# Second layer norm and router logits of a vision-transformer tower: logits token by token, rows normalised on ScalarE, moments a block ahead

## The chip, the cores and the metric

The program runs on one core of a Trainium2 chip. The metric is the device time of one execution in microseconds (us); the median of a few runs is quoted. The engines of a core are TensorE (PE; its weight loads are shown as PEld), VectorE (DVE), ScalarE (ACT), GpSimd (POOL) and SyncE (SP), which here issues the DMA transfers.

## The reference

64 images give 12544 tokens of 256 channels. A token embedding is followed by a 16-head attention block and then by a feed-forward block of one shared expert and eight routed ones, each block on a layer-normed copy of the rows. The change lies in what stands ahead of the feed-forward block:

```python
m = jnp.mean(x, axis=axis, keepdims=True)
v = jnp.var(x, axis=axis, keepdims=True)
return (x - m) / jnp.sqrt(v + eps)
...
z = xf @ proj_w.T + proj_b
s = jax.nn.sigmoid(z) + expert_bias
```

`x` are the rows h1 that attention left in DRAM (12544 x 256, f32), `xf` the normed rows, `proj_w` is 8 x 256. Then come the choice of two experts per token, the capacity cut of each expert, and the experts.

## The kernel before

The program is a row of stages with a barrier after each: `project` (embedding, first layer norm, Q, K, V), `attend`, `route`, and three `feed_forward` stages. The change touches `route` alone. Each engine has its own instruction list in the source; what orders them are semaphores, and inside an engine the order is as written.

`route` first walks over the tokens in 28 blocks of 4 tiles of 112 tokens (`BLOCKS`, `BLOCK`, `GROUP`; N = 448 tokens), and then works out the expert tables from the logits of all tokens, `z`. The walk is the function `position(n, u)`, once per engine, called for n from -2 to 27; the middle positions run in a hardware loop of two. In one position the engines do this:

- SP waits for the normed rows of block n+2, loads the input of block n+4 (L1563) into the buffer that they came from, and stores the normed rows (L1581).
- DVE takes the moments of block n+2 (`bn_stats` L1654, `bn_aggr` L1660, four each), waits for ScalarE's square root, takes the reciprocal (L1663), writes the normed rows `xf` (L1668, four instructions), and last adds the bias to the logits of block n (L1673).
- ACT takes the square root for block n+2 (L1602), copies the 8 x 448 logits of block n+1 out of PSUM (`zT`, L1606), and copies the transposed rows of block n+2 out of PSUM (`xT`, L1609).
- PE multiplies for block n+1 with the 128 x 8 router weights as the stationary operand and the 448 tokens streaming (`psZ`, L1842, two f32 products, each two records in the trace), turns the logits of block n back to token-major with four small transposes (`psB`, L1849), and transposes the rows of block n+2 with eight (`psT`, L1856).

`xT` and `psT` are single buffers: the transposes of a block wait until `xT` of the block before has been copied (L1609), and that copy waits for the transposes of its own block. `hin` (the input) and `xf` have two buffers each. In the rest of the text Z is the product into `psZ`, B the small transposes into `psB`, and T the eight transposes into `psT`. Two other places of the program are read for their durations: L469 in `project`, eight products with `prod` (128 x 98 tokens) as the stationary operand and 8 streaming columns, sixteen records in all, and L1868 in `route`, a 128 x 128 stationary operand with one column.

Of the kernel before, what the change touches and what calls it, by code (L numbers as in the profile page):

```python
# [20 lines left out]
C = 256  # L21
# [1006 lines left out]
BLOCK = 4  # L1028
# [439 lines left out]
def route(nc, d, networks):  # L1468
# [5 lines left out]
    with stage(nc) as ctx:  # L1474
# [12 lines left out]
        def plain(x):  # L1487
# [9 lines left out]
        hin = [sb(f"hin{u}", [GROUP, BLOCK, C]) for u in range(2)]  # L1497
        xf = [sb(f"xf{u}", [GROUP, BLOCK, C]) for u in range(2)]
        stats, mv = sb("stats", [GROUP, BLOCK, 6]), sb("mv", [GROUP, BLOCK, 2])
        std, rstd = sb("std", [GROUP, BLOCK]), sb("rstd", [GROUP, BLOCK])  # L1500
        xT, zT = sb("xT", [128, 2, N]), sb("zT", [EXPERTS, N])
# [22 lines left out]
        psZ, psB, psC = pb("psZ", [EXPERTS, 512]), pb("psB", [GROUP, BLOCK, EXPERTS]), pb("psC", [GROUP, EXPERTS])  # L1524
# [8 lines left out]
        h_in, xf_out = transfers("h1_in"), transfers("xf_out")  # L1533
        stats_ok, mv_ok, std_ok, rstd_ok, xf_ok = (signal(x) for x in ("stats", "mv", "std", "rstd", "xf"))
        t_ok, xT_ok, z_ok, zT_ok, zz_ok, zw_ok = (signal(x) for x in
                                                 ("xT_in_psum", "xT", "z_in_psum", "zT", "z_transposed", "z"))
# [9 lines left out]
        def positions(eng, position):  # L1546

            for n in (-2, -1, 0, 1):
                position(n, n % 2)
            with eng.Fori(1, BLOCKS // 2 - 2) as j:  # L1550
                for u in range(2):
                    position(j * 2 + u, u)
            for n in range(BLOCKS - 4, BLOCKS):
                position(n, n % 2)

        with nc.Block() as block:
            @block.sync
            def _(sp):
                for s in (h_in, xf_out):
                    s.open(sp)  # L1560

                def load(n, u):
                    sp.dma_start(hin[u][:], tiles_of(d["h1"][bass.ds(n * N, N), :], GROUP)).then_inc(h_in.sems[u], 16)  # L1563

                load(0, 0)
                load(1, 1)
                for dst, name in ((ident, "ident"), (wz, "proj_w"), (bz, "proj_b"), (eb, "expert_bias"), (iota, "iota"),
                                  (rows0, "rows0"), (tri32, "tri"), (blk8, "blk8")):
                    sp.dma_start(dst[:], d[name]).then_inc(setup, 16)

                for x, raw in zip(networks, raws):
                    for dst, src in ((raw[0], "w1"), (raw[1], "w2"), (x.b1, "b1"), (x.b2, "b2")):
                        sp.dma_start(dst[:], d[x.source + src][0]).then_inc(w_in, 16)

                def position(n, u):
                    if known(n, -2, BLOCKS - 2):
                        sp.wait_ge(xf_ok.sem, xf_ok.at(n + 2))
                        sp.sem_inc(passed["sp"], 1)
                        if known(n, -2, BLOCKS - 4):
                            load(n + 4, u)  # L1580
                        sp.dma_start(tiles_of(d["xf"][bass.ds((n + 2) * N, N), :], GROUP), xf[u][:]).then_inc(xf_out.sems[u], 16)  # L1581

                positions(sp, position)
                sp.wait_ge(xf_out.sems[0], xf_out.at(BLOCKS - 2, 0))
                sp.wait_ge(xf_out.sems[1], xf_out.at(BLOCKS - 1, 1))

                sp.wait_ge(tables_ready, 1)
                for name, src in (("gidx", gidx), ("gw", gw), ("sidx", sidx)):
                    sp.dma_start(d[name], src[:]).then_inc(tables_out, 16)
                sp.wait_ge(tables_out, 48)  # L1590

            @block.scalar
            def _(act):
                for s in (std_ok, xT_ok, zT_ok):
                    s.open(act)
                act.wait_ge(made, 1)

                def position(n, u):
                    if known(n, -2, BLOCKS - 2):
                        act.wait_ge(mv_ok.sem, mv_ok.at(n + 2))  # L1600
                        act.wait_ge(rstd_ok.sem, rstd_ok.at(n + 1))
                        act.activation(std[:], mv[:, :, 1], ACT.Sqrt, bias=eps[:, 0:1]).then_inc(std_ok.sem, 1)  # L1602
                    if known(n, -1, BLOCKS - 1):
                        act.wait_ge(z_ok.sem, z_ok.at(n + 1))
                        act.wait_ge(zz_ok.sem, zz_ok.at(n))
# [26 lines left out]
            def _(dve):  # L1632
                for s in (stats_ok, mv_ok, rstd_ok, xf_ok, zw_ok):
                    s.open(dve)
# [15 lines left out]
                def position(n, u):  # L1650
                    if known(n, -2, BLOCKS - 2):
                        dve.wait_ge(h_in.sems[u], h_in.at(n + 2, u))
                        for t in range(BLOCK):
                            last = nc.vector.bn_stats(stats[:, t, :], hin[u][:, t, :])  # L1654
                        last.then_inc(stats_ok.sem, 1)
                        dve.wait_ge(stats_ok.sem, stats_ok.at(n + 2))
                        dve.wait_ge(std_ok.sem, std_ok.at(n + 1))
                        dve.sem_inc(passed["dve"], 1)
                        for t in range(BLOCK):
                            last = nc.vector.bn_aggr(mv[:, t, :], stats[:, t, :])  # L1660
                        last.then_inc(mv_ok.sem, 1)
                        dve.wait_ge(std_ok.sem, std_ok.at(n + 2))
                        nc.vector.reciprocal(rstd[:], std[:]).then_inc(rstd_ok.sem, 1)  # L1663
                        dve.wait_ge(rstd_ok.sem, rstd_ok.at(n + 2))
                        dve.wait_ge(xf_out.sems[u], xf_out.at(n, u))
                        dve.wait_ge(t_ok.sem, t_ok.at(n))
                        for t in range(BLOCK):
                            last = nc.vector.tensor_scalar(xf[u][:, t, :], hin[u][:, t, :], mv[:, t, 0:1], rstd[:, t:t + 1],  # L1668
                                                           ALU.subtract, ALU.mult)
                        last.then_inc(xf_ok.sem, 1)  # L1670
                    if known(n, 0, BLOCKS):
                        dve.wait_ge(zz_ok.sem, zz_ok.at(n))
                        nc.vector.tensor_tensor(z[:, bass.ds(n * BLOCK, BLOCK), :], psB[:],  # L1673
                                                         bz[:].unsqueeze(1).broadcast_to([GROUP, BLOCK, EXPERTS]), ALU.add).then_inc(zw_ok.sem, 1)
# [156 lines left out]
            def _(pe):  # L1831
                for s in (t_ok, z_ok, zz_ok):
# [4 lines left out]
                def position(n, u):  # L1837
                    if known(n, -1, BLOCKS - 1):
                        pe.wait_ge(xT_ok.sem, xT_ok.at(n + 1))
                        pe.wait_ge(zT_ok.sem, zT_ok.at(n))  # L1840
                        for h in range(2):
                            last = nc.tensor.matmul(psZ[:, 0:N], wz[:, h, :], xT[:, h, :], start=(h == 0), stop=(h == 1))  # L1842
                        last.then_inc(z_ok.sem, 1)
                    if known(n, 0, BLOCKS):
                        pe.wait_ge(zT_ok.sem, zT_ok.at(n))
                        pe.wait_ge(zw_ok.sem, zw_ok.at(n - 1))
                        pe.sem_inc(passed["pe"], 1)
                        for t in range(BLOCK):
                            last = nc.tensor.transpose(psB[:, t, :], zT[:, t * GROUP:(t + 1) * GROUP], ident[0:EXPERTS, 0:EXPERTS])  # L1849
                        last.then_inc(zz_ok.sem, 1)  # L1850
                    if known(n, -2, BLOCKS - 2):
                        pe.wait_ge(xf_ok.sem, xf_ok.at(n + 2))
                        pe.wait_ge(xT_ok.sem, xT_ok.at(n + 1))
                        for h in range(2):
                            for t in range(BLOCK):
                                last = nc.tensor.transpose(psT[:, h, t * GROUP:(t + 1) * GROUP], xf[u][:, t, h * 128:(h + 1) * 128],  # L1856
# [137 lines left out]
```

## Time and profile before

| | us |
|---|---|
| median of 3 runs | 3623.16 (3621.2 to 3627.92) |
| the profiled execution, time | 3636.08 |
| the profiled execution, span | 3634.4 |

The page of the profiled execution gives busy times, shares of the span and instruction counts of the engines:

```profile
span 3634.4 us, 89293 instructions
PE 3229.9 (89%) x34825; PEld 2526.0 (70%) x34881; DVE 2623.7 (72%) x6129; ACT 1498.6 (41%) x2991; POOL 1617.8 (45%) x1965
```

The 40 equal slices of the span (90.9 us each) show the stages; a digit is a tenth of busy time, 9 is 90% or more, and PEclk is the granted clock of TensorE in tenths of full speed:

```profile
PE   6999999399999999999996722999599999998997
DVE  5888888568888888888884676554266666665887
ACT  3444444056666666666663310332133333332221
PEclk9999999579999999999998855999799999998999
```

The walk of `route` lies in slices 22 and 23 (counted from 1), 1966 to 2110 us; the work on the tables follows to 2250 us. What the profile calls the granted clock is 1.00 at 2.4 GHz and 0.50 at 1.2 GHz.

### The profile page before, as it was taken

What the parts mean: (1) busy time and instruction counts of PE and PEld (TensorE: products, weight loads), DVE (VectorE), ACT (ScalarE), POOL (GpSimd) and SP (SyncE); (2) the same over time, 40 slices, a digit from 0 to 9 for tenths busy, and PEclk for the clock granted to TensorE, in tenths of its full rate; (3) what the DMA queues carried; (4) which work ended last, traced back from release to release, by engine and by line L of the source; (5) the groups of instructions that cost most, each with busy time, mean ns of one, the idle gap of its engine ahead of it and who ended that gap; (6) DMA issues with size and microseconds to landing.
All of it is one profiled execution on the core that took longest, in us unless ns stands there. A gap on an engine that the chain in (4) does not pass through costs nothing. (4 is left out here: it accounts for less than half of the span.)

```text
span 3634.4 us, 89293 instructions
## 1 busy us (share of the span) xinstructions
PE 3229.9 (89%) x34825; PEld 2526.0 (70%) x34881; DVE 2623.7 (72%) x6129; ACT 1498.6 (41%) x2991; POOL 1617.8 (45%) x1965
## 2 busy tenths in 40 slices
PE   6999999399999999999996722999599999998997
PEld 6888887378888888888883311778377777775876
DVE  5888888568888888888884676554266666665887
ACT  3444444056666666666663310332133333332221
POOL 2555555256666666666662010577200000004776
PEclk9999999579999999999998855999799999998999
DMA  4666665736556565665654611354333333225776
GB/s 141 185 185 197 195 186 161 189 84 164 157 149 172 136 166 148 160 162 148 170 133 131 182 30 34 110 140 126 95 116 111 107 104 106 95 90 135 217 219 165
DMA packets 449244, 518.11 MB, mean 143 GB/s; under 512 B 64150, under 2 KB 418804, under 8 KB 448397
## 3 DMA queue, kind: packets, MB, share of 16 engines
q1 hardware_dynamic: 427376, 473.19, 46.1%
q0 software_dynamic: 21504, 39.94, 4.1%
q8 instruction: 245, 4.01, 0.5%
q14 instruction: 119, 0.97, 0.1%
HBM read 306.93 MB, written 215.94 MB: 144 GB/s over the span
## 5 line engine op out<-in xcount | busy, mean ns | idle before, releaser
L1281 POOL DMA_INDIRECT sb_ye<-scratch_ye,sb_table x224 | 240.8, 1075 | 805.6 <-DMA sb_gw<-scratch_gw 733.3
L854 DVE TENSOR_REDUCE p_mx<-p_psS 98x2 f32<-98x390 f32 (+1 forms) x1024 | 527.1, 556 | 0.0
L800 ACT ACTIVATE p_after<-p_psF 98x392 f32<-98x392 f32 x512 | 255.1, 498 | 480.6 <-PE p_psF L946 472.5
L803 ACT ACTIVATE p_probs<-p_psE 98x392 f32<-98x392 f32 x1024 | 450.1, 496 | 0.0
L848 DVE COPY_PREDICATED p_psS<-p_later,p_psD 98x196 f32<-98x196 uint32 x1024 | 330.6, 362 | 120.0 <-PE p_psS L932 111.4
L749 POOL TENSOR_SCALAR_AFFINE_SELECT p_after<-p_after 98x392 f32<-98x392 f32 x512 | 274.4, 536 | 243.2 <-ACT p_after L800 243.0
L1269 POOL DMA_INDIRECT scratch_xe<-sa_xs,sa_table x224 | 222.2, 992 | 205.6 <-DMA sa_xs<-scratch_xf 140.4
L753 POOL TENSOR_SCALAR_AFFINE_SELECT p_probs<-p_probs 98x392 f32<-98x392 f32 x512 | 274.5, 536 | 85.8 <-ACT p_probs L803 80.2
L969 PE MATMUL p_psO<-p_probs,p_v 98*32 98x196 f32 x4096 | 279.8, 345 | 2.0 <-POOL p_probs L753 1.7
L419 POOL TENSOR_TENSOR p_rt<-p_rt 128x784 f32<-128x784 f32 x64 | 187.1, 2924 | 122.7 <-DVE p_st L397 122.7
L103 PE MATMUL p_psH<-p_wh,p_xh 128*98 128x256 bf16 x768 | 211.5, 275 | 24.3 <-DVE p_xl L334 24.3
L916 PE MATMUL p_psD<-p_K,p_U 96*98 96x98 bf16 (+1 forms) x2048 | 187.8, 215 | 36.7 <-DVE p_later L835 29.0
L916 PEld LDWEIGHTS p_psD<-p_K,p_U 96*98 96x98 bf16 x2048 | 160.6, 128 | 73.4 <-DVE p_later L835 29.1
L103 PE MATMUL p_psH<-p_wl,p_xh 128*98 128x256 bf16 x768 | 211.3, 275 | 0.0
L103 PE MATMUL p_psH<-p_wh,p_xl 128*98 128x256 bf16 x768 | 211.2, 275 | 0.0
L946 PE MATMUL p_psF<-p_U,p_K 98*98 98x98 bf16 x2048 | 180.3, 211 | 28.8 <-DMA p_U<-p_mrow 28.8
L1387 DVE CAST ex_gh<-ex_g 128x512 bf16<-128x512 f32 (+1 forms) x256 | 106.3, 415 | 106.7 <-ACT ex_g L1322 87.4
L973 PE MATMUL p_psO<-p_after,p_v 98*32 98x98 f32 x4096 | 182.3, 250 | 0.0
L1389 DVE TENSOR_TENSOR ex_gl<-ex_g,ex_gh 128x512 bf16<-128x512 f32 (+1 forms) x256 | 171.4, 669 | 8.8
L1322 ACT ACTIVATE ex_g<-ex_psG,ex_b 128x512 f32<-128x512 f32 (+1 forms) x128 | 85.7, 669 | 219.7 <-PE ex_psG L103 219.7
L1322 ACT ACTIVATE ex_g<-ex_psG,ex_first_b 128x512 f32<-128x512 f32 (+1 forms) x128 | 85.7, 669 | 218.1 <-PE ex_psG L103 218.1
L946 PEld LDWEIGHTS p_psF<-p_U,p_K 98*98 98x98 bf16 x2048 | 147.5, 127 | 32.5 <-DMA p_U<-p_mrow 31.6
(300 smaller groups left out, 10110.7 us busy)
## 6 DMA issues: line engine op xcount, KB each, us to landing
scratch_stack<-p_st SPq DMA_DIRECT2D x64, 784.0 KB, 6.0
p_x<-in_x SPq DMA_DIRECT2D x32, 1176.0 KB, 9.5
p_L<-scratch_stack SPq DMA_DIRECT2D x192, 196.0 KB, 4.3
p_U<-scratch_stack SPq DMA_DIRECT2D x192, 196.0 KB, 4.4
scratch_xe<-p_zero SPq DMA_DIRECT2D x32, 1024.0 KB, 5.9
ex_xin<-scratch_xe SPq DMA_DIRECT2D x56, 512.0 KB, 4.0
scratch_ye<-ex_y SPq DMA_DIRECT2D x56, 512.0 KB
scratch_h<-p_h SPq DMA_DIRECT2D x32, 392.0 KB
```

Of the source, the lines that this page charges most:

```text
L103: last = nc.tensor.matmul(out, a, b, start=start and k == 0, stop=stop and k == len(todo) - 1)
L749: nc.gpsimd.affine_select(after[c][:], after[c][:], pattern=[[0, 4], [-1, TILE]], compare_op=ALU.is_ge, fill=nothing, base=-2, channel_mul ...
L753: nc.gpsimd.affine_select(diagonal, diagonal, pattern=[[0, 4], [1, TILE]], compare_op=ALU.is_ge, fill=nothing, base=0, channel_multiplier= ...
L800: act.activation(after[c][:].rearrange("p h t -> p (h t)"), psF[:, 0:4 * TILE], ACT.Exp, scale=DK ** -0.5).then_inc(p_ok.sem, 1)
L803: act.activation(probs[c][:, b, :], psE[:, b, 0:PAIR], ACT.Exp, scale=DK ** -0.5).then_inc(p_ok.sem, 1)
L848: nc.vector.copy_predicated(own[:, :, c * TILE:(c + 1) * TILE], later[:].unsqueeze(1).broadcast_to([TILE, 2, TILE]), upper).then_inc(chose ...
L854: nc.vector.tensor_reduce(mx[g1][:, c, 4 * q1 + 2 * b:4 * q1 + 2 * b + 2], own, AX.X, ALU.max).then_inc(s_max.sem, 1)
L916: last = nc.tensor.matmul(psD[:, j * TILE:j * TILE + wide], U[u][0:STACK, h][:, mid], K[u][0:STACK, h][:, mid.start + 1:mid.start + 1 + wi ...
L946: last = nc.tensor.matmul(psF[:, j * TILE:(j + 1) * TILE], K[u][0:ROWS, h][:, mid], U[u][0:ROWS, h][:, mid], start=True, stop=True)
L969: nc.tensor.matmul(psO[32 * j:32 * j + 32, 0:S], v32[u][:, 2 * g + c, 4 * q + j, :], probs[c][:, j // 2, (j % 2) * S:(j % 2 + 1) * S], sta ...
L1269: nc.gpsimd.indirect_dma_start(out=d["xe"], out_offset=bass.IndirectOffsetOnAxis(ap=table[:, b * BLOCK + t, k:k + 1], axis=0), in_=xs[v][: ...
L1281: nc.gpsimd.indirect_dma_start(out=ye[v][u][:, t, k, :], out_offset=None, in_=d["ye"], in_offset=bass.IndirectOffsetOnAxis(ap=table[:, at ...
```

## The change

All of it is in the walk of `route`.

- **Logits.** The operands of Z change places: the transposed rows `xT`, 112 tokens at a time, are now the stationary operand, and the 8 columns of `wz` stream. That makes 8 products per block in place of 2, and the result is already token-major, so B, the copy `zT` on ScalarE and their semaphores go. `psZ` is now 112 x 4 x 8 and has two buffers.
- **Rows.** `xf` is written by ScalarE, `rstd * h - mean * rstd`, four instructions with a bias and a scale per partition. DVE makes `nmr = -mean * rstd` with one small instruction after the reciprocal.
- **Order.** The moments are taken at position n for block n+4, the rows are written for block n+3; so positions run from -4. On ScalarE the order in a position is rows of n+3, square root of n+4, copy `xT` of n+2. On PE it is Z of n+1, T of n+3. Small buffers (`mv`, `std`, `rstd`, `nmr`) are double.
- **Input.** Four `hin` buffers; blocks 2 and 3 are loaded before the experts' weights, and a load is issued for n+7 at position n.
- **Loop.** The hardware loop is gone; all positions are written out.

```diff
-        hin = [sb(f"hin{u}", [GROUP, BLOCK, C]) for u in range(2)]
+        hin = [sb(f"hin{v}", [GROUP, BLOCK, C]) for v in range(4)]
...
-            for n in (-2, -1, 0, 1):
-                position(n, n % 2)
-            with eng.Fori(1, BLOCKS // 2 - 2) as j:
...
+            for n in range(-4, BLOCKS):
                 position(n, n % 2)
...
+                    if known(n, -3, BLOCKS - 3):
+                        v = 1 - u
+                        act.wait_ge(rstd_ok.sem, rstd_ok.at(n + 3))
+                        act.wait_ge(xf_out.sems[v], xf_out.at(n + 1, v))
+                        act.wait_ge(t_ok.sem, t_ok.at(n + 1))
+                        for t in range(BLOCK):
+                            last = act.activation(xf[v][:, t, :], hin[(n + 3) % 4][:, t, :], ACT.Identity, bias=nmr[v][:, t:t + 1],
+                                                  scale=rstd[v][:, t:t + 1])
+                        last.then_inc(xf_ok.sem, 1)
...
-                        act.activation(zT[:], psZ[:, 0:N], ACT.Copy).then_inc(zT_ok.sem, 1)
                     if known(n, -2, BLOCKS - 2):
                         act.wait_ge(t_ok.sem, t_ok.at(n + 2))
+                        act.wait_ge(z_ok.sem, z_ok.at(n + 1))
                         act.activation(xT[:], psT[:, :, 0:N], ACT.Copy).then_inc(xT_ok.sem, 1)
...
+                        nc.vector.scalar_tensor_tensor(nmr[v][:], mv[v][:, :, 0], -1.0, rstd[v][:], ALU.mult, ALU.mult).then_inc(rstd_ok.sem, 1)
...
-                        for t in range(BLOCK):
-                            last = nc.vector.tensor_scalar(xf[u][:, t, :], hin[u][:, t, :], mv[:, t, 0:1], rstd[:, t:t + 1],
-                                                           ALU.subtract, ALU.mult)
-                        last.then_inc(xf_ok.sem, 1)
...
                         pe.wait_ge(xT_ok.sem, xT_ok.at(n + 1))
-                        pe.wait_ge(zT_ok.sem, zT_ok.at(n))
-                        for h in range(2):
-                            last = nc.tensor.matmul(psZ[:, 0:N], wz[:, h, :], xT[:, h, :], start=(h == 0), stop=(h == 1))
+                        pe.wait_ge(zw_ok.sem, zw_ok.at(n - 1))
+                        for t in range(BLOCK):
+                            for h in range(2):
+                                last = nc.tensor.matmul(psZ[1 - u][:, t, :], xT[:, h, t * GROUP:(t + 1) * GROUP], wz[:, h, :],
+                                                        start=(h == 0), stop=(h == 1))
                         last.then_inc(z_ok.sem, 1)
-                    if known(n, 0, BLOCKS):
-                        pe.wait_ge(zT_ok.sem, zT_ok.at(n))
-                        pe.wait_ge(zw_ok.sem, zw_ok.at(n - 1))
                         pe.sem_inc(passed["pe"], 1)
-                        for t in range(BLOCK):
-                            last = nc.tensor.transpose(psB[:, t, :], zT[:, t * GROUP:(t + 1) * GROUP], ident[0:EXPERTS, 0:EXPERTS])
-                        last.then_inc(zz_ok.sem, 1)
```

## Rows read from the trace of the kernel before

**Rows 1.** Windows over the walk: length, busy of five engines, granted clock, DMA share, GB/s.
```profile
1966.00:2109.60 143.60, 98.36 (x448) 41.90 (x448) 96.78 (x394) 51.30 (x86) 0.00 (x0) 0.85 0.64 195
```
**Rows 2.** Timeline, two neighbouring blocks: start, length, engine, line, operation, [idle before <-releaser].
```profile
2095.82 1.67 PE L1842 MATMUL p_psZ<-p_xT,p_wz 128*8 128x448 f32 x4 [1.01 <-ACT p_xT L1609]
2097.41 0.38 PE L1849 MATMUL p_psB<-p_ident,p_zT 8*112 8x8 f32 x4
2098.22 0.99 PE L1856 MATMUL p_psT<-p_ident,p_xf 112*128 112x112 f32 x8 [0.43 <-DVE p_xf L1668]
2099.25 0.92 ACT L1609 ACTIVATE p_xT<-p_psT 128x896 f32<-128x896 f32 x1 [0.82 <-PE p_psT L1856]
...
2100.22 3.01 PE L1842 MATMUL p_psZ<-p_xT,p_wz 128*8 128x448 f32 x4 [1.01 <-ACT p_xT L1609]
...
2103.16 0.54 PE L1849 MATMUL p_psB<-p_ident,p_zT 8*112 8x8 f32 x4
2103.63 1.05 PE L1856 MATMUL p_psT<-p_ident,p_xf 112*128 112x112 f32 x8
```
**Rows 3.** Waits in the walk: who waited for whom, total us, times, longest us.
```profile
PE p_psZ L1842 <- ACT p_xT L1609: 29.1, 28, 1.1
PE p_psT L1856 <- DVE p_xf L1668: 8.6, 13, 0.9
DVE p_stats L1654 <- DMA p_hin<-scratch_h: 1.0, 2, 0.7
```
**Rows 4.** Timeline, start of the walk: the first T, copy and Z, and their neighbours.
```profile
1966.50 1.40 DVE L1654 BATCH_NORM_STATS2 p_stats<-p_hin 112x6 f32<-112x256 f32 x4
1968.08 0.38 DVE L1660 BATCH_NORM_AGGREGATE p_mv<-p_stats 112x2 f32<-112x6 f32 x4 [0.17 <-DVE p_stats L1654]
1969.82 0.30 ACT L1602 ACTIVATE p_std<-p_mv,p_eps 112x4 f32<-112x4 f32 x1
1970.15 0.18 DVE L1663 RECIPROCAL p_rstd<-p_std 112x4 f32<-112x4 f32 x1 [1.70 <-ACT p_std L1602]
...
1972.01 1.73 PE L1856 MATMUL p_psT<-p_ident,p_xf 112*128 112x112 f32 x8 [20.45 <-DVE p_xf L1668]
1973.77 0.92 ACT L1609 ACTIVATE p_xT<-p_psT 128x896 f32<-128x896 f32 x1 [3.65 <-PE p_psT L1856]
1974.74 3.03 PE L1842 MATMUL p_psZ<-p_xT,p_wz 128*8 128x448 f32 x4 [1.01 <-ACT p_xT L1609]
```
**Rows 5.** Timeline, end of the walk.
```profile
2105.69 1.67 PE L1842 MATMUL p_psZ<-p_xT,p_wz 128*8 128x448 f32 x4 [1.01 <-ACT p_xT L1609]
...
2109.61 0.95 ACT L1613 ACTIVATE p_c<-p_z 112x896 f32<-112x896 f32 x1
```
**Rows 6.** Timeline of PE in `project`: L469 at clock 0.50, then at 1.00.
```profile
639.67 2.83 PE L469 MATMUL p_psT<-p_blk,p_prod 128*98 128x8 f32 x16 [6.34 <-DVE p_nl L363]
202.33 1.47 PE L469 MATMUL p_psT<-p_blk,p_prod 128*98 128x8 f32 x16
```
**Rows 7.** Timeline of PE in the tables: one product, 128 x 128 stationary, one column.
```profile
2134.14 0.58 PE L1868 MATMUL p_psK<-p_count_of,p_same 128*128 128x1 f32 x2 [2.05 <-DVE p_hits L1742]
```
**Rows 8.** Windows of PE alone in the walk: length, busy (records), granted clock, DMA share, GB/s.
```profile
1970.80:1974.10 3.30, 1.73 (x8) 0.50 1.04 374
1974.20:1977.50 3.30, 2.76 (x4) 0.50 0.95 286
1977.60:1981.00 3.40, 2.39 (x13) 1.00 0.87 245
...
1998.10:2001.40 3.30, 1.38 (x10) 1.00 0.49 121
2001.50:2004.80 3.30, 3.30 (x11) 0.50 0.83 246
```
**Rows 9.** Windows of PE alone in `project` (L469) and `attend`.
```profile
639.60:642.90 3.30, 3.23 (x19) 0.50 0.59 180
643.00:646.30 3.30, 3.30 (x17) 0.50 0.08 8
656.70:660.00 3.30, 2.23 (x14) 0.50 0.82 249
660.10:663.40 3.30, 0.51 (x4) 0.50 0.08 8
740.00:760.00 20.00, 20.00 (x223) 0.50 0.17 55
```
**Rows 10.** Groups of ACT: count, busy us, mean ns, idle before.
```profile
L309 ACT ACTIVATE p_st<-p_psJ,p_cols 128x392 bf16<-128x392 f32 x64 | 37.6, 587 | 53.6 <-PE p_psJ L103 53.6
L1606 ACT ACTIVATE p_zT<-p_psZ 8x448 f32<-8x448 f32 x28 | 14.9, 534 | 57.4 <-PE p_psB L1849 54.5 <-PE p_psZ L1842 2.9
```

More of the change, by code:

```diff
@@ L1496, in route @@
         tri, ones = sb("tri", [GROUP, GROUP], BF16), sb("ones", [GROUP, GROUP], BF16)
-        hin = [sb(f"hin{u}", [GROUP, BLOCK, C]) for u in range(2)]
+        hin = [sb(f"hin{v}", [GROUP, BLOCK, C]) for v in range(4)]
         xf = [sb(f"xf{u}", [GROUP, BLOCK, C]) for u in range(2)]
-        stats, mv = sb("stats", [GROUP, BLOCK, 6]), sb("mv", [GROUP, BLOCK, 2])
-        std, rstd = sb("std", [GROUP, BLOCK]), sb("rstd", [GROUP, BLOCK])
-        xT, zT = sb("xT", [128, 2, N]), sb("zT", [EXPERTS, N])
+        stats, mv = sb("stats", [GROUP, BLOCK, 6]), [sb(f"mv{u}", [GROUP, BLOCK, 2]) for u in range(2)]
+        std, rstd, nmr = ([sb(f"{x}{u}", [GROUP, BLOCK]) for u in range(2)] for x in ("std", "rstd", "nmr"))
+        xT = sb("xT", [128, 2, N])
         z, c, key, oh1, oh2, c2, w, t1, t2 = (sb(x, wide) for x in
@@ L1523, in route @@
         psT = pb("psT", [128, 2, 512])
-        psZ, psB, psC = pb("psZ", [EXPERTS, 512]), pb("psB", [GROUP, BLOCK, EXPERTS]), pb("psC", [GROUP, EXPERTS])
+        psZ, psC = [pb(f"psZ{u}", [GROUP, BLOCK, EXPERTS]) for u in range(2)], pb("psC", [GROUP, EXPERTS])
         psK = pb("psK", [128, 512])
@@ L1532, in route @@
         setup, made = plain("constants_loaded"), plain("constants_made")
[L1533 to L1536, printed above, removed]
+        h_in, xf_out = [plain(f"h1_in{v}") for v in range(4)], transfers("xf_out")
+        stats_ok, mv_ok, std_ok, recip_ok, rstd_ok, xf_ok = (signal(x) for x in ("stats", "mv", "std", "reciprocal", "rstd_and_shift", "xf"))
+        t_ok, xT_ok, z_ok, zw_ok = (signal(x) for x in ("xT_in_psum", "xT", "z_in_psum", "z"))
         sig_ok = plain("sigmoid")
@@ L1558, in _, with load @@
             def _(sp):
[L1559 to L1566, printed above, removed]
+                xf_out.open(sp)
+                def load(n):
+                    sp.dma_start(hin[n % 4][:], tiles_of(d["h1"][bass.ds(n * N, N), :], GROUP)).then_inc(h_in[n % 4], 16)
+                load(0)
+                load(1)
                 for dst, name in ((ident, "ident"), (wz, "proj_w"), (bz, "proj_b"), (eb, "expert_bias"), (iota, "iota"),
@@ L1569, in _ @@
                     sp.dma_start(dst[:], d[name]).then_inc(setup, 16)
+                load(2)
+                load(3)
                 for x, raw in zip(networks, raws):
@@ L1593, in _ @@
             def _(act):
-                for s in (std_ok, xT_ok, zT_ok):
+                for s in (std_ok, xf_ok, xT_ok):
                     s.open(act)
@@ L1598, in position @@
                 def position(n, u):
[L1599 to L1605, printed above, removed]
-                        act.activation(zT[:], psZ[:, 0:N], ACT.Copy).then_inc(zT_ok.sem, 1)
+                    if known(n, -3, BLOCKS - 3):
+                        v = 1 - u
[6 more added lines that the diff above has]
+                        last.then_inc(xf_ok.sem, 1)
+                    if known(n, -4, BLOCKS - 4):
+                        act.wait_ge(mv_ok.sem, mv_ok.at(n + 4))
+                        act.wait_ge(rstd_ok.sem, rstd_ok.at(n + 2))
+                        act.activation(std[u][:], mv[u][:, :, 1], ACT.Sqrt, bias=eps[:, 0:1]).then_inc(std_ok.sem, 1)
                     if known(n, -2, BLOCKS - 2):
                         act.wait_ge(t_ok.sem, t_ok.at(n + 2))
+                        act.wait_ge(z_ok.sem, z_ok.at(n + 1))
                         act.activation(xT[:], psT[:, :, 0:N], ACT.Copy).then_inc(xT_ok.sem, 1)
@@ L1632, in _ @@
             def _(dve):
-                for s in (stats_ok, mv_ok, rstd_ok, xf_ok, zw_ok):
+                for s in (stats_ok, mv_ok, recip_ok, rstd_ok, zw_ok):
                     s.open(dve)
@@ L1650, in position @@
                 def position(n, u):
-                    if known(n, -2, BLOCKS - 2):
-                        dve.wait_ge(h_in.sems[u], h_in.at(n + 2, u))
+                    if known(n, -3, BLOCKS - 3):
+                        v = 1 - u
+                        dve.wait_ge(std_ok.sem, std_ok.at(n + 3))
+                        dve.wait_ge(xf_ok.sem, xf_ok.at(n + 1))
+                        nc.vector.reciprocal(rstd[v][:], std[v][:]).then_inc(recip_ok.sem, 1)
+                        dve.wait_ge(recip_ok.sem, recip_ok.at(n + 3))
+                        nc.vector.scalar_tensor_tensor(nmr[v][:], mv[v][:, :, 0], -1.0, rstd[v][:], ALU.mult, ALU.mult).then_inc(rstd_ok.sem, 1)
@@ L1653, in position @@
+                    if known(n, -4, BLOCKS - 4):
+                        v = (n + 4) % 4
+                        dve.wait_ge(h_in[v], 16 * ((n + 4) // 4 + 1))
+                        dve.wait_ge(mv_ok.sem, mv_ok.at(n + 3))
                         for t in range(BLOCK):
-                            last = nc.vector.bn_stats(stats[:, t, :], hin[u][:, t, :])
+                            last = nc.vector.bn_stats(stats[:, t, :], hin[v][:, t, :])
                         last.then_inc(stats_ok.sem, 1)
-                        dve.wait_ge(stats_ok.sem, stats_ok.at(n + 2))
@@ L1657, in position @@
-                        dve.wait_ge(std_ok.sem, std_ok.at(n + 1))
+                        dve.wait_ge(stats_ok.sem, stats_ok.at(n + 4))
+                        dve.wait_ge(rstd_ok.sem, rstd_ok.at(n + 2))
                         dve.sem_inc(passed["dve"], 1)
                         for t in range(BLOCK):
-                            last = nc.vector.bn_aggr(mv[:, t, :], stats[:, t, :])
+                            last = nc.vector.bn_aggr(mv[u][:, t, :], stats[:, t, :])
                         last.then_inc(mv_ok.sem, 1)
-                        dve.wait_ge(std_ok.sem, std_ok.at(n + 2))
@@ L1670, in position @@
-                        last.then_inc(xf_ok.sem, 1)
                     if known(n, 0, BLOCKS):
-                        dve.wait_ge(zz_ok.sem, zz_ok.at(n))
-                        nc.vector.tensor_tensor(z[:, bass.ds(n * BLOCK, BLOCK), :], psB[:],
-                                                         bz[:].unsqueeze(1).broadcast_to([GROUP, BLOCK, EXPERTS]), ALU.add).then_inc(zw_ok.sem, 1)
+                        dve.wait_ge(z_ok.sem, z_ok.at(n))
+                        nc.vector.tensor_tensor(z[:, n * BLOCK:(n + 1) * BLOCK, :], psZ[u][:],
+                                                bz[:].unsqueeze(1).broadcast_to([GROUP, BLOCK, EXPERTS]), ALU.add).then_inc(zw_ok.sem, 1)
@@ L1831, in _ @@
             def _(pe):
-                for s in (t_ok, z_ok, zz_ok):
+                for s in (t_ok, z_ok):
                     s.open(pe)
```

24 lines of the change are left out of this document (8 added, 16 removed).

## The prediction

> **What bounds the kernel now.** I read the windows first. The walk takes 143.6 us, 4% of the span, and in it no engine is full: PE 98.36 us, DVE 96.78, ACT 51.30, DMA share 0.64, granted clock 0.85 [rows 1]. So latencies round a loop set the pace, and the timeline shows which: Z, B and T follow one another on PE, the copy `xT` (0.92 us) waits for T, and the next Z waits for that copy [rows 2]. From the first Z at 1974.74 [rows 4] to the last at 2105.69 [rows 5] there are 27 periods in 130.95 us, 4.85 us each. The waits agree: PE stood 29.1 us for `xT` (28 times, the 0.92 us and hand-overs) and only 8.6 us for DVE's rows [rows 3]. Periods come in two kinds. At clock 1.00 Z takes 1.67 us and a period 4.40 (2095.82 to 2100.22, with 0.43 us of waiting for rows); at 0.50 Z takes 3.01 and the period is 5.47 (2100.22 to 2105.69) [rows 2, 5]. The reader should see that PE plus the copy is the loop, DVE is second with small waits, and the clock is the large term.
>
> **Which clock the new work gets.** This decides the sum, so it comes first. In before, the stage begins at 0.50; eight transposes alone (1.73 us busy) left it there; after a Z of long streams it rose to 1.00 for T, B and Z; after a stretch with the late start of a Z and otherwise only transposes (1.38 us busy) it fell [rows 8]. So it is the 448-column streams of Z that bring the clock up, and the change takes just these away: new Z streams 16 times 8 columns. The nearest rows to that are L469, sixteen records with 8 streaming columns, at 0.50: after 14 of them (2.23 us busy) and after all 16 with a few others (3.23 of 3.30 us busy) the next stretch was still at 0.50. In `attend` PE was busy for 20.00 of 20.00 us at 0.50, so a busy record does not raise it by itself [rows 9]. I therefore take 0.50 for the whole walk. The Trainium skill (TensorE: Matmul & The Clock Gate, Part 4) says that transposes do not count as busy for the clock; by that rule too T could not bring it up, and the first T above, which left the clock at 0.50, agrees.
>
> **The change, part by part, per block.**
>
> B goes: 0.38 us at 1.00, 0.54 at 0.50 [rows 2]. Copy `zT` (0.534 us, rows 10) lay beside PE and on nobody's path but B's; its removal gives ScalarE room only.
>
> Z, new: 16 records with a stationary operand of 128 x 112 and 8 columns. L469 has the same form with 98 token columns: 2.83 us for 16 at 0.50, 1.47 at 1.00 [rows 6]. Loading the stationary operand sets this, since the streams are 8 columns; it scales with token columns: the 128-column product has two records in 0.58 us, so a spacing of about 0.22 against (2.83 - 0.34) / 15 = 0.166 for 98 columns, taking 0.34 for the last record [rows 6, 7]. For 112 columns I scale 2.83 by 112/98 to 3.2 us. Bounds: 2.83 (no scaling) and 16 x 0.215 = 3.44. At 1.00 it would be 1.47 x 112/98 = 1.7, the same as the old Z's 1.67. So the exchange of operands is free at full clock and, without clock, costs what the old slow Z cost (3.03, rows 4).
>
> T is unchanged, at 0.50 it takes 1.73 us [rows 4], 0.99 at 1.00 [rows 2]. Z's first load begins about 0.26 us before T's last record ends (spacing 0.183, last record some 0.45), so T's share before Z is 1.47; bound 1.73.
>
> Copy `xT`: 0.92 us, now on both T of its block and Z of the block before; hand-overs 0.05 before and 0.08 after it [rows 2]. PE now does T(n+2), Z(n+1), and waits for `xT`(n+2), so the period is 1.47 + 3.2 + 0.03 + 0.92 + 0.13 = 5.75 us against 4.85.
>
> What lies beside that period: ScalarE writes four row tiles. The nearest row, 128x392 with one per-partition operand, takes 587 ns [rows 10]; 136 elements fewer at 0.855 ns (from 917 ns for 896 and 534 for 448 elements, rows 2, 10) gives 470 ns. With overlap or a second operand I take 1.9 to 2.2 us for four; plus the square root, 0.30. Queued behind them on ScalarE is `xT`(n+2), which waits 4.7 us for PE anyway, so this costs nothing; if PE ran at full clock (T + Z = 2.5 us), 2.5 us of ScalarE would just fill it. DVE loses four row instructions and has 1.40 + 0.38 + 0.18 plus a small one for `nmr` (0.18, by the reciprocal) and the bias add: under 3 us, hidden. The wait for rows (8.6 us in all, rows 3) disappears; it is within the 4.85. DMA moves the same bytes in a longer period, and the earlier loads remove at most 1.0 us of waiting [rows 3]. On SP a load for n+7 stands ahead of the store as before and both wait only for the rows. Loop instructions go; written out, they lie behind PE's waits: nothing, with at most 3 us either way.
>
> **Sum.** 27 periods x (5.75 - 4.85) = +24.3 us. Start: before, the first `xT` ended at 1974.69. Now ScalarE does rows(0), then rows(1) and the square root of block 2 before it: square root(0) to 1970.12, reciprocal and `nmr` to 1970.75, rows(0) to 1972.8, square root(1) to 1973.1, `nmr`(1) 1973.8, rows(1) 1975.8, square root(2) 1976.1, `xT`(0) to 1977.05: +2.4. End: before, 3.92 us from the last Z's start to the sigmoid [rows 5]; now Z 3.2, bias add 0.2, hand-over 0.1: -0.4. Together +26.3. Against the profiled execution's own 3636.08 that is 3662.4; it stands 12.9 above the median of the runs, so by the median 3623.16 + 26.3 = 3649.5 us, +0.73%. Bounds from Z (-10, +6.5) and T (+7) and 3 us for code and runs: 3637 to 3664.
>
> **Rivals.**
>
> *The clock is 1.00 as soon as PE has shorter gaps.* Then Z is 1.7, T's share 0.8: a period of 0.8 + 1.7 + 0.95 + 0.13 = 3.6; ScalarE's 2.2 + 0.3 + 0.92 with hand-overs is about as long, so 3.7. 27 x (3.7 - 4.85) = -31, start and end +1: 3593, faster. Everything hangs on TensorE's clock: PE's work per period is denser than before (gaps of 1.1 us only), which speaks for it; rows 8 and 9 speak against. The turn is at a period of about 4.8, so with half of the blocks at each clock (5.75 and 3.7, mean 4.7) the gain is gone.
>
> *The clock alternates as it does before.* Then 27 x (4.7 - 4.85) + 2 = -2: 3621, no change.
>
> *A load is shorter than I take it.* At 0.50, if a load took as long as it does at 1.00 (1.47 / 16 = 0.09 us a record, rows 6), Z would be 1.7 us and the period 4.25: 27 x (-0.6) + 1 = -15, 3608. The Trainium skill (TensorE: Matmul & The Clock Gate, Part 2, LDWEIGHTS) gives a load as columns divided by 1.2 in ns, 93 ns for 112 columns, whatever the clock, which is this case. L469 took nearly twice as long at 0.50 as at 1.00, so the trace contradicts it for f32.
>
> *The change does not unload PE at all in the sense that counts:* DVE's rows and the input buffers were worth 8.6 + 1.0 us at most [rows 3]; this part does what it says but is covered by PE's longer phase. That is part of the forecast.
>
> **How the numbers follow.** Chance of the forecast (0.50 throughout) 0.84; clock 1.00 throughout 0.05; alternating 0.07; short loads 0.04. A measurement of this kernel can tell about 0.2%, 7 us, from no change. Slower by over that: 0.83; within: 0.07; faster: 0.10. The range 3637 to 3664 is that of the forecast and holds it nine times in ten; the other cases are left out as they are less than 2 in 10.
>
> **What would show it.** After: granted clock 0.50 in all windows of the walk, Z near 3.2 us for 16 records, T 1.73, a period of 5.75, no wait of PE for rows, the walk some 26 us longer, and ScalarE waiting for PE ahead of `xT`. It is wrong if the windows show 1.00 (then look for periods of 3.7), if Z's sixteen records take under 2.5 us at 0.50, or if `xT` waits behind the row instructions of ScalarE rather than for PE.

## The result

| | us |
|---|---|
| before, median of 4 runs | 3625.54 (3621.2 to 3629.04) |
| after, median of 4 runs | 3654.69 (3651.31 to 3658.19) |
| after / before | 1.0081, 95% interval 1.0065 to 1.0097 |
| profiled execution of after, time (span) | 3656.93 (3655.2) |

The change makes the kernel 0.81% slower; 3649.5 us and +0.73% were forecast. The page of after (parts 1 and 2, engines by line) stands against the one of before:

```profile
PE 3255.7 (89%) x35049; PEld 2608.3 (71%) x35105; DVE 2586.8 (71%) x6045; ACT 1533.9 (42%) x3075; POOL 1618.8 (44%) x1965
...
PE   6999999499999999999995732999599999998997
...
DVE  5888888478888888888873366555266666665987
ACT  3444444056666666666664510332133333332221
...
PEclk9999999589999999999995555999799999998999
```

DVE lost 36.9 us of busy time and ScalarE gained 35.3, as the change means to; TensorE's weight loads gained 82 us. The clock digits of slices 22 and 23 went from 8 and 8 to 5 and 5. The stretch from the first moments to the sigmoid is the walk. Windows over it (busy of PE, PEld, DVE, ACT, POOL with records, then granted clock, DMA share, GB/s), whole and without its first blocks:

```profile
1958.20:2127.50 169.30, 127.50 (x672) 125.34 (x672) 62.45 (x309) 88.70 (x170) 0.00 (x0) 0.50 0.54 164
1980.00:2127.50 147.50, 117.26 (x619) 115.45 (x619) 50.73 (x253) 76.50 (x146) 0.00 (x0) 0.50 0.48 143
```

In before it ran from 1966.50 to 2109.61 [rows 4, 5], 143.1 us at 0.85 [rows 1]; now it takes 169.3 us at 0.50: +26.2 us. The rest of the difference is outside the change: in the two profiled executions the part ahead of the walk was 8.3 us shorter after the change (1958.2 against 1966.5) and the part behind it 2.9 us longer (1527.7 against 1524.8), though its code is the same. In the fourteen profiled kernels of this study the part ahead spread from 1953.7 to 1966.5 us. So below I read the walk from traces and the sign of a change from the ratio of runs. The low clock is not that of one execution: averaged over the whole span it was 0.922 to 0.924 in the four runs of after, and 0.938 to 0.944 in the runs of before that went with the experiments.

One block of after in the timeline (start, length, engine, line, operation, [idle before <-releaser]):

```profile
1981.47 2.06 ACT L1600 ACTIVATE p_xf<-p_hin,p_nmr,p_rstd 112x256 f32<-112x256 f32 x4
1981.69 1.41 PEld L1853 LDWEIGHTS p_psT<-p_ident,p_xf 112*128 112x128 f32 x8 [1.22 <-issue]
1981.72 1.73 PE L1853 MATMUL p_psT<-p_ident,p_xf 112*128 112x112 f32 x8 [1.16 <-ACT p_xT L1610]
1983.05 3.11 PEld L1844 LDWEIGHTS p_psZ<-p_wz,p_xT 128*112 128x112 f32 x16
1983.24 3.02 PE L1844 MATMUL p_psZ<-p_wz,p_xT 128*112 128x8 f32 x16
1983.43 0.29 ACT L1606 ACTIVATE p_std<-p_mv,p_eps 112x4 f32<-112x4 f32 x1
1986.36 0.92 ACT L1610 ACTIVATE p_xT<-p_psT 128x896 f32<-128x896 f32 x1 [2.63 <-PE p_psZ L1844]
```

The next T starts at 1987.42, 5.70 us after this one. The weight loads of Z fill 3.11 us, the eight-column streams hide behind them, and ScalarE, done with its rows and its square root at 1983.72, stands 2.63 us until Z is done. The waits (who for whom: us in total, times, longest) say the same of the walk from 1975 us on:

```profile
ACT p_xT L1610 <- PE p_psZ L1844: 70.8, 26, 4.8
...
PE p_psT L1853 <- ACT p_xT L1610: 32.2, 26, 3.3
```

PE no longer waits for rows behind the first block (8.6 us in rows 3). The long wait is now ScalarE's for PE, ahead of `xT`.

### The profile page after: what moved, and what is told of

It is laid out like the page before. It is cut to its first block and busy times, and to the rows that moved or that the text cites. A ratio compares the mean times of both kernels' runs of the same rounds, so it can differ in the third digit from the quotient of the medians.

```text
span 3655.2 us, 89450 instructions
## 1 busy us (share of the span) xinstructions
PE 3255.7 (89%) x35049; PEld 2608.3 (71%) x35105; DVE 2586.8 (71%) x6045; ACT 1533.9 (42%) x3075; POOL 1618.8 (44%) x1965
## 5 line engine op out<-in xcount | busy, mean ns | idle before, releaser
L916 PEld LDWEIGHTS p_psD<-p_K,p_U 96*98 96x98 bf16 x2048 | 160.1, 128 | 72.6 <-DVE p_later L835 29.2
```

The lines of the kernel that those rows point to most:

```text
L916: last = nc.tensor.matmul(psD[:, j * TILE:j * TILE + wide], U[u][0:STACK, h][:, mid], K[u][0:STACK, h][:, mid.start + 1:mid.start + 1 + wi ...
```

## The experiments

The theory: TensorE's clock stays at 0.50 because the change takes the long streams of Z away; at that clock Z costs its sixteen weight loads, and they lie on the chain. Rivals: rows on ScalarE or the new order are the cost; the clock has nothing to do with the streams; the stretch has another limit right behind. Every ratio is against the kernel before on the same chip.

### The logits alone, in the kernel before

```diff
-                        for h in range(2):
-                            last = nc.tensor.matmul(psZ[:, 0:N], wz[:, h, :], xT[:, h, :], start=(h == 0), stop=(h == 1))
+                        for t in range(BLOCK):
+                            for h in range(2):
+                                last = nc.tensor.matmul(psZ[1 - u][:, t, :], xT[:, h, t * GROUP:(t + 1) * GROUP], wz[:, h, :],
+                                                        start=(h == 0), stop=(h == 1))
```

> The kernel before with the logits part alone: xT stationary, 8 columns streaming, no zT and no small transposes; DVE still writes the rows, two input buffers, hardware loop. Theory: clock 0.50 throughout, the same PE loop of T 1.47 + Z 3.0 + xT 0.92 and hand-overs, DVE's 4.2 us per block hidden in it: period 5.7, time within 4 us of the changed kernel (3650 to 3658). Rival A (the order of the change costs too): clearly less than that, by 5 us or more. Rival C (the loop and DVE's rows add to the longer PE phase): over 3660.

Measured: 3657.57 us, ratio 1.0076 (1.006 to 1.0093), the same as the whole change (1.0081). The walk:

```profile
1961.10:2131.80 170.70, 132.07 (x672) 123.10 (x672) 94.09 (x393) 33.52 (x58) 0.00 (x0) 0.50 0.54 161
```

170.7 us at 0.50 with DVE still at 94 us, against 169.3: this part alone brings all of the loss, and the rows and the order of the change give back next to nothing while PE is this long. Inside they are not quite without effect. A block takes 5.90 us here (T at 1989.91 and 1995.81 in the timeline) against the 5.70 expected and measured in after; after loses most of those 27 x 0.2 us again in its first blocks, as told below.

### Half of the products

```diff
-                            for h in range(2):
+                            for h in range(1):
                                 last = nc.tensor.matmul(psZ[1 - u][:, t, :], xT[:, h, t * GROUP:(t + 1) * GROUP], wz[:, h, :],
-                                                        start=(h == 0), stop=(h == 1))
+                                                        start=True, stop=True)
```

This leaves out half of the channels, so the logits are others; only the walk is read from it.

> The changed kernel with the second half of the channels left out of the logits (4 products per block, 8 records instead of 16), so the logits are of half the channels. Theory (Z is priced by its loads at 0.50 and lies wholly on the chain): 8 x 0.19 = 1.5 us less per block, period 5.70 to 4.2, the walk 41 us shorter, time 3613. Rival (another wait is right behind): less than 30 us.

Measured: 3617.28 us, ratio 0.9965 (0.9954 to 0.9975). The window over the walk:

```profile
1955.90:2085.70 129.80, 85.69 (x448) 83.53 (x448) 59.88 (x309) 88.79 (x171) 0.00 (x0) 0.50 0.72 214
```

The clock is 0.50 as in after, but the walk is 39.5 us shorter than 169.3, against 41 forecast, and a block takes 4.21 us against 4.2. The loads of Z, at the price of the low clock, lie on the chain nearly one for one.

### Unread streams on TensorE

Products that nobody reads, 448 bf16 columns each, behind Z in the changed kernel; first four per block, then eight.

```diff
                         last.then_inc(z_ok.sem, 1)
                         pe.sem_inc(passed["pe"], 1)
+                        for _ in range(8):
+                            nc.tensor.matmul(psU[:, 0, 0:448], ones[:], stream[:], start=True, stop=True)
```

> The changed kernel plus four bf16 products per block with 448 streaming columns (112x112 ones stationary) behind Z on PE, whose results nobody reads; they fill the stretch in which PE waits for xT. Theory: streams are what the clock lacks. If four (0.75 us at 1.00) are enough, clock 1.00, T share 0.83, Z 1.6, period 3.5 to 3.7, time near 3598. If they are too few, they cost 4 x 0.373 = 1.5 us at 0.50 in a gap of 1.1: period 6.1, time near 3666. Rival (clock does not follow streams): the second outcome here and with eight too.

> As with four streams, but eight per block. Theory: clock 1.00, the eight take 1.5 us of PE, 0.4 us more than the gap: period 3.9 to 4.1, time near 3610. Rival (clock does not follow streams): 8 x 0.373 = 3.0 us at 0.50, period 7.6, time near 3705.

Measured: with four, 3647.36 us, ratio 1.0044 (1.0029 to 1.006), the walk 160.0 us; with eight, 3612.18 us, ratio 0.9959 (0.9944 to 0.9974), the walk 124.3 us. Windows, with four (the first three quarters of the walk) and with eight (before and after the clock rose):

```profile
1957.00:1997.00 40.00, 29.42 (x142) 26.14 (x142) 18.44 (x92) 21.50 (x42) 0.00 (x0) 0.50 0.78 238
1997.00:2037.00 40.00, 38.57 (x231) 33.62 (x231) 17.53 (x92) 25.17 (x49) 0.00 (x0) 0.67 0.67 196
2037.00:2077.00 40.00, 39.28 (x213) 34.64 (x211) 15.29 (x77) 23.73 (x48) 0.00 (x0) 0.59 0.58 169
```

```profile
1960.90:1988.00 27.10, 18.09 (x80) 14.92 (x81) 13.27 (x66) 15.26 (x30) 0.00 (x0) 0.50 0.89 278
1988.40:2085.20 96.80, 96.74 (x809) 84.19 (x810) 46.44 (x243) 74.44 (x140) 0.00 (x0) 1.00 0.72 209
```

Four streams gave a clock that came and went, between the two outcomes written down: blocks of 5.88 us at 0.50 and single blocks of 3.61 us (T at 2003.38 and 2006.99) at 1.00. Eight held it at 1.00 from 1988 us to the end of the walk. A block of that part, eight streams:

```profile
2033.17 0.93 PE L1857 MATMUL p_psT<-p_ident,p_xf 112*128 112x112 f32 x8
...
2033.94 1.65 PE L1846 MATMUL p_psZ<-p_wz,p_xT 128*112 128x8 f32 x16
...
2035.45 1.70 PE L1851 MATMUL p_psU<-p_stream,p_ones 112*112 112x448 bf16 x8
```

Z's sixteen records take 1.65 us in place of 3.02, T 0.93 in place of 1.73; 1.5 us of work for nothing per block make the block 1.9 us shorter (3.81 against 5.70). That is the clearest evidence: more work, less time, and what differs is the clock. It does not show that the added products had to be long streams: the same busy time in short ones was not tried. Busy time alone is not what does it, since PE stood at 0.50 while busy for 20.00 of 20.00 us [rows 9].

### The same in the kernel before

Four such products behind T in the kernel before.

> The kernel before plus four bf16 products of 448 streaming columns per block behind T, in the 1.0 us in which PE waits for xT. Theory (the alternating clock costs the kernel before 27 x 0.6 us): clock 1.00, period 4.2 to 4.3, set by DVE, time 16 us under the kernel before. Rival (the clock's falls in the kernel before are hidden by DVE or DMA): no change within 5 us.

Measured: 3618.59 us, ratio 0.9965 (0.9951 to 0.9979). From 1985 us on the clock is 1.00, and the walk is 130.4 us against 143.1:

```profile
1985.00:2089.80 104.80, 87.19 (x472) 41.74 (x470) 77.92 (x316) 41.72 (x70) 0.00 (x0) 1.00 0.68 201
```

So the alternating clock did cost the kernel before some 13 us, of 16 forecast. Blocks now take 3.93 and 4.94 us in turn, 4.43 in the mean (forecast 4.2 to 4.3). In the longer ones PE waits for the rows (0.89 us ahead of the T at 2035.97); so DVE, with its four row instructions, its four moments and the waits for the square root between, seems to set the pace; no run tests it.

### The logits put back, rows and order kept

The changed kernel with Z, `zT` and B of before.

> The changed kernel with the logits part undone: router weights stationary, 448 tokens streaming, zT and the four small transposes back; rows by ScalarE, order and buffers of the change stay. Theory (the lost streams cost the clock): granted clock 1.00 for most of the walk, Z 1.67 us, period T 0.83 + Z 1.6 + zT 0.5 + xT 0.92 + hand-overs 0.15 = 4.0 us against 5.70; the walk shortens by 27 x 1.7 = 46 us, time near 3609 and so below the kernel before (by 27 x 0.85 = 23 us). Rival A (rows on ScalarE and the new order are the cost): time stays near 3650. Rival B (clock falls all the same): periods of 5.3 to 5.5 us, time near 3645.

Measured: 3680.84 us, ratio 1.0137 (1.0117 to 1.0156): slower than the change itself. All three expectations missed. In the four runs the clock averaged over the span was 0.923 to 0.927, as low as in after. The windows show why, in three stretches:

```profile
1960.90:2009.00 48.10, 27.59 (x110) 12.13 (x111) 20.71 (x104) 29.38 (x59) 0.00 (x0) 0.71 0.75 233
2009.30:2135.40 126.10, 97.42 (x295) 40.75 (x293) 38.97 (x201) 63.28 (x129) 0.00 (x0) 0.50 0.43 128
2135.50:2150.80 15.30, 9.57 (x44) 3.79 (x44) 0.77 (x4) 7.38 (x13) 0.00 (x0) 0.89 0.11 31
```

For 126 us the clock stayed at 0.50 although every block had a Z with its full streams; ahead of and behind that stretch it changed, with single blocks of 4.44 us at 1.00 (T at 2136.55 and 2140.99). A block of the long stretch:

```profile
2026.91 1.73 PE L1861 MATMUL p_psT<-p_ident,p_xf 112*128 112x112 f32 x8 [1.57 <-ACT p_xT L1614]
...
2028.57 3.15 PE L1847 MATMUL p_psZ<-p_xT,p_wz 128*8 128x448 f32 x4
...
2031.65 0.54 PE L1854 MATMUL p_psB<-p_ident,p_zT 8*112 8x8 f32 x4
...
2032.29 0.53 ACT L1611 ACTIVATE p_zT<-p_psZ 8x448 f32<-8x448 f32 x1 [3.37 <-PE p_psB L1854]
...
2032.73 0.89 ACT L1614 ACTIVATE p_xT<-p_psT 128x896 f32<-128x896 f32 x1
```

Here the order of the change hurts: T comes ahead of Z on PE, so `xT` can only follow Z, B and `zT`, in one chain of 6.85 us. The expectation had `zT` in the chain, but not B, and it had the clock at 1.00. B and `zT` together explain at most 1.2 us of a block (0.54, 0.53 and hand-overs); the rest is the clock. Streams in each block are thus not enough to bring it up. What in this loop keeps it down is left open. So each half of the change keeps the clock low without the other: the new logits in the old order (walk 170.7 us), and here the new rows and order with the old logits.

### The copy `xT` ahead of `zT`

The same kernel with the two copies on ScalarE exchanged; the wait for Z, which `zT` had covered, now stands ahead of `xT` too.

```diff
-                    if known(n, -1, BLOCKS - 1):
-                        act.wait_ge(z_ok.sem, z_ok.at(n + 1))
-                        act.wait_ge(zz_ok.sem, zz_ok.at(n))
-                        act.activation(zT[:], psZ[:, 0:N], ACT.Copy).then_inc(zT_ok.sem, 1)
                     if known(n, -2, BLOCKS - 2):
                         act.wait_ge(t_ok.sem, t_ok.at(n + 2))
+                        act.wait_ge(z_ok.sem, z_ok.at(n + 1))
                         act.activation(xT[:], psT[:, :, 0:N], ACT.Copy).then_inc(xT_ok.sem, 1)
+                    if known(n, -1, BLOCKS - 1):
+                        act.wait_ge(z_ok.sem, z_ok.at(n + 1))
+                        act.wait_ge(zz_ok.sem, zz_ok.at(n))
+                        act.activation(zT[:], psZ[:, 0:N], ACT.Copy).then_inc(zT_ok.sem, 1)
```

> The changed kernel with the old logits, and on ScalarE the copy xT(n+2) ahead of zT(n+1) instead of behind it. In e1_old_logits every period is a chain T 1.5, Z 3.1, B 0.5, zT 0.45, xT 0.9 and hand-overs, 6.85 us at clock 0.50. Theory: B and zT leave the chain, so 5.65 us where the clock is 0.50 and 3.65 where it is 1.00; time 3649 if it stays at 0.50, 3595 if it comes up. Rival (the small transposes or the rows set the 6.85): nothing gained.

Measured: 3610.08 us, ratio 0.9948 (0.9931 to 0.9964). The walk is 124.3 us in place of 189.9, and its later part runs at 1.00:

```profile
1953.70:1980.00 26.30, 14.85 (x46) 7.08 (x47) 12.10 (x60) 16.02 (x32) 0.00 (x0) 0.50 0.87 277
1980.50:2078.00 97.50, 72.12 (x402) 33.43 (x400) 48.72 (x249) 84.90 (x167) 0.00 (x0) 1.00 0.72 208
```

Two copies exchanged give 65.6 us of walk. The runs agree: ratios of 1.0137 and 0.9948, and an average clock of 0.942 in all four runs here against 0.923 to 0.927. In the early part, at 0.50, a block takes 5.98 us (T at 1971.00 and 1976.98 in its timeline) against 6.85, so the chain alone would give 27 x 0.87 = 23 us, less than the 1.2 us a block that I had forecast; the other two thirds came with the clock. At 1.00 a block takes 3.82 us in the mean (T from 1985.98 to 2069.93, 22 blocks), and ScalarE is busy 84.9 of 97.5 us: it is the next bound.

### Streams with the logits put back

> e1_old_logits plus four bf16 products of 448 streaming columns per block behind B, in the 1.6 us in which PE waits for zT and xT; nothing reads them. Theory (e1_old_logits is slow by a clock that its own gaps keep low): the clock is 1.00, the chain 0.83 + 1.6 + 0.38 + 0.5 + 0.9 + 0.2 = 4.4 us, the walk 65 us shorter than e1_old_logits, time near 3616. Rival (the order alone makes it slow): the clock rises but the gain stays under 30 us, or the clock stays and nothing changes, 3681.

Four products as above behind B. Measured: 3626.35 us, ratio 0.999 (0.9981 to 1.0); the walk 139.6 us, 50 less than without streams, where 65 were forecast:

```profile
1955.30:1978.00 22.70, 10.81 (x32) 4.98 (x32) 10.00 (x50) 12.54 (x25) 0.00 (x0) 0.51 0.93 299
1978.00:2094.90 116.90, 99.38 (x529) 46.95 (x528) 50.65 (x260) 87.93 (x173) 0.00 (x0) 1.00 0.61 180
```

With the clock up and the chain as it was, a block takes 4.44 us (T at 2033.37 and 2037.81 in its timeline), against 4.4 worked out. So the two causes in the kernel with old logits come apart: 2.4 us per block were the clock (6.85 to 4.44), about 0.6 more the chain (to 3.82 in the kernel above). The forecast of 65 us took 27 blocks at 6.85 against 27 at 4.4; but the first blocks here ran at 0.50, and the kernel without streams had some blocks at 1.00.

### The start of the walk

Four kernels tried to save the slow first blocks. The first is the kernel with eight streams plus 44 while PE waits for the constants, and eight behind each of the first two T.

> e4_streams_8 plus 44 such products while PE waits for the constants, and eight each behind the first two T. In e4_streams_8 the first blocks ran at 0.50 with periods of 8.3 and 7.4 us against 3.8 later. Theory: all blocks at 1.00, 8 to 12 us less than e4_streams_8, time near 3602. Rival (the start is set by the moments and the DMA, not by PE): less than 3 us gained.

Measured: 3612.75 us, ratio 0.9942 (0.9924 to 0.996), not apart from the 0.9959 without; the walk of the profiled execution was even longer, 136.0 us. That execution, at 3620.19 us, was the slowest of four that lie far apart; the two fastest, 3603.95 and 3608.75 us, had an average clock of 0.946 against its 0.942. So what follows is one execution's, and the fastest came near the 3602 us expected. The windows:

```profile
1957.40:1976.80 19.40, 13.10 (x85) 9.48 (x84) 9.07 (x44) 10.52 (x21) 0.00 (x0) 1.00 0.96 295
1976.90:2007.50 30.60, 30.60 (x137) 25.65 (x136) 11.07 (x57) 13.83 (x28) 0.00 (x0) 0.50 0.50 150
2007.70:2093.30 85.60, 85.33 (x712) 73.81 (x712) 39.93 (x210) 64.91 (x122) 0.00 (x0) 1.00 0.71 205
```

The clock was up at the start and fell after one wait, which the timeline shows:

```profile
1973.26 2.07 ACT L1601 ACTIVATE p_xf<-p_hin,p_nmr,p_rstd 112x256 f32<-112x256 f32 x4 [6.00 <-DMA scratch_xf<-p_xf]
...
1976.47 1.53 PE L1860 MATMUL p_psT<-p_ident,p_xf 112*128 112x112 f32 x8 [3.55 <-ACT p_xT L1611]
```

ScalarE may not write the third block's rows until the store of the first has landed, and that store ran beside the loads of the experts' weights, in a stretch with a DMA share of 0.96. PE stood 3.55 us. After that the clock stayed at 0.50 for 30.6 us although PE was busy for all of them. So the next two move those loads behind the walk, in the changed kernel and in the kernel with `xT` first; the last one adds the products at the start to the second of them:

```diff
-                for x, raw in zip(networks, raws):
-                    for dst, src in ((raw[0], "w1"), (raw[1], "w2"), (x.b1, "b1"), (x.b2, "b2")):
-                        sp.dma_start(dst[:], d[x.source + src][0]).then_inc(w_in, 16)
...
                 positions(sp, position)
+                for x, raw in zip(networks, raws):
+                    for dst, src in ((raw[0], "w1"), (raw[1], "w2"), (x.b1, "b1"), (x.b2, "b2")):
+                        sp.dma_start(dst[:], d[x.source + src][0]).then_inc(w_in, 16)
```

> The changed kernel with the experts' weights (3.2 MB) loaded after the walk instead of before it. In the changed kernel ScalarE stood 4.8 us at the third block until the first store of rows had landed, beside those loads. Theory: that stall goes, the walk is 3 to 5 us shorter (169 to 165); the tables stage has 20 us before it needs the weights, so nothing is given back: time 3651. Rival (the stall is hidden by TensorE at 0.50): no change of the walk.

> e5_xT_first with the weights loaded after the walk. Theory: 4 us of stall go, and with denser first blocks the clock comes up earlier; the walk 124 to 116 us, time 8 us under e5_xT_first. Rival (the clock comes up by chance, not by order): the walk stays between 120 and 150 us.

> e10_xT_first_late plus 44 unread products of 448 columns while PE waits for the constants and eight behind each of the first two T. In e8_warm_start the clock had come up before the walk and was lost in a 3.5 us wait of PE that the late store caused. Theory: with that wait gone the clock stays at 1.00 from the first block: 28 periods of 3.8 and a start and end of 10, the walk 112 us, time near 3600. Rival (the start cannot hold the clock): as e10_xT_first_late.

Measured: the changed kernel with late weights has a ratio of 1.0061 (1.004 to 1.0081), not apart from 1.0081; its walk is 167.3 us, 2.1 less where 3 to 5 were forecast. ScalarE still stood 1.97 us for the first store at the third block, of 4.8 before, and the period from the second T to the third is 5.70 in place of 7.82: 2 us of the stall had been on the path. The kernel with `xT` first and late weights: 3608.09 us, ratio 0.9932 (0.9912 to 0.9952), walk 118.9 against 124.3 (116 forecast); by their ratios the two are not apart. With the streams at the start as well: 3607.63 us, ratio 0.9934 (0.9914 to 0.9955), walk 118.6. Its clock was 1.00 from 1960 us on, as expected, and yet nothing more was gained. The 112 us expected were mis-summed (28 x 3.8 + 10 is 116.4), and without the products at the start the clock was already at 0.99 from 1978 us, 13 us into the walk. Two stretches of the kernel with the products at the start:

```profile
1970.00:1980.00 10.00, 7.80 (x42) 3.67 (x41) 4.66 (x26) 8.07 (x17) 0.00 (x0) 1.00 0.78 231
...
2000.00:2020.00 20.00, 14.35 (x80) 6.72 (x80) 11.47 (x59) 18.48 (x38) 0.00 (x0) 1.00 0.83 240
```

ScalarE is busy 18.48 of 20 us. With the clock up it is ScalarE, not PE, that sets the period of 3.81 us in the mean (T from 1978.52 to 2069.97, 24 blocks; 3.72 where its instructions follow one another without a gap), so a clock that is up sooner has little left to give. The version with `xT` first and the weights late beats both kernels, by 0.68% against before.

## Why the prediction was right

- **The clock** was forecast at 0.50 for the whole walk, from L469 and the first T [rows 8, 9]. It was 0.50 in every window. The eight-stream kernel shows that the clock is the cause: with it at 1.00, Z took 1.65 us (forecast for 1.00: 1.7) and the loss was gone. But the statement behind it, that the streams bring the clock up, holds only half: no walk here rose without them, and the kernel with old logits shows that they are not enough. The prediction did not see that the new order can hold the clock down even with them.
- **Z** at 0.50: 3.2 us forecast by scaling L469 [rows 6], 3.02 measured, 3.11 for its loads. The last Z, which like L469 starts on an idle PE, took 3.15 us, so the scaling was fair; the others save the first load, which runs beside the end of T. The loads are 0.19 us apart at 0.50 and 0.10 at 1.00. The Trainium skill (TensorE: Matmul & The Clock Gate, Part 2, LDWEIGHTS) gives a load as its columns divided by 1.2 in ns, 93 ns for 112, and names no clock, which the prediction took as one price at both; it comes near the spacing at 1.00 and is half of the one at 0.50. The rival of loads as short at 0.50 as at 1.00, 3608 us, fell.
- **T**: 1.73 us at 0.50, from its start to Z's 1.52 (forecast 1.47). **Period**: 5.70 against 5.75; 27 of them come to +23 us (forecast +24.3). The mean of 4.85 us for before is right, but its "two kinds" of period are not: from T to T the trace of before shows everything from 3.90 to 5.52 us behind the first block.
- **ScalarE's rows**: 2.06 us for four (forecast 1.9 to 2.2), in the shadow of PE; DVE under 3 us (1.40, 0.38, 0.18, 0.16 and 0.19 us in a block), also in it. Neither appears in the time to speak of, as forecast: the logits alone took 1.4 us more of walk than everything.
- **The start** was mis-sized: `xT`(0) ended 9.9 us after the first moments against 8.2 before, +1.7 (forecast +2.4), but the wait of the third block's rows for the first store was not foreseen. From the start of `xT`(0) to that of `xT`(1) it took 7.84 us, 2.1 more than a period. The prediction had said that on SP nothing changes for the stores; it missed that ScalarE now waits for them with the weights' loads beside. **The end**: 3.41 us against 3.92, -0.5 (forecast -0.4).
- The sum of the walk, +26.2 us, is the +26.3 forecast, with the errors of period (-1.3) and start (+1.4, the stall included) cancelling; that the sum agrees to 0.1 us is luck. Of the runs' +29.2 the other 3 are not explained; the parts outside the walk spread by more than that. The upper end of the range does not follow from its own terms: 6.5 + 7 + 3 above 3649.5 is 3666, not 3664; the measured 3654.69 lies inside either way.
- **The rival of a full clock** was priced at a period of 3.7 us. The four streams reached 3.61 in single blocks at 1.00 and the eight 3.81 with the surplus work, so the price was fair and only the condition was not met.

## What to carry to other kernels

Before exchanging the operands of a product so that few columns stream, price it at TensorE's low clock: look for rows of the same shape at 0.50, and ask what in the new loop would bring the clock up. When a loop through two engines is the bound, the order of two copies on the second engine can be worth more than the work removed (65.6 us of walk here for an exchange, two thirds of it through the clock). Relieving an engine that is not on the chain gives next to nothing by itself: DVE's 36.9 us moved for 1.4 us of walk. A forecast of a low clock can come true for more than one reason; only the kernels that put one part back at a time told them apart.

## What was not expected of the hardware

- Two walks, one mostly at full clock and one mostly at half, differed by the order of two copies on another engine: 124.3 and 189.9 us, with the same work and the same streams. The kernel that stayed low had full streams in every block of 6.85 us.
- TensorE busy for 30.6 of 30.6 us, eight unread streams in each block included, stayed at 0.50 after a single wait of 3.55 us, and then rose to 1.00 under the same load (the profiled execution of the kernel with products at the start). In what state of the loop it rises is open.
- Work without use made the kernel faster: eight unread products a block, 1.5 us of TensorE's time, gave 1.9 us per block; four gave a clock of 0.50 to 0.67 in stretches of 40 us and a walk of 160.0 us.
